# Decoder stack of twelve sections on one core: the attention shift in two bf16 parts instead of three, its selectors in four row tiles, masks behind them, and a new order of turns

## Chip, core and metric

The kernel runs on one NeuronCore of a Trainium2 chip. The metric is the device time of one execution in microseconds; the number given for a kernel is the median of its runs. The kernel before took 4295.11 us (median of 3 runs, 4294.72 to 4298.41).

## What is computed

Input `x` is 32 sequences of 128 tokens of width 128. Four layers follow, each of an attention, a cross attention and a feed-forward part, each behind a layer norm and added to `x`:

```python
x = x + _L0_attn_ref(_layernorm(x, axis=-1), ...)     # delta rule
x = x + _L0_xattn_ref(_layernorm(x, axis=-1), ctx_1024, ctx_1024, ...)   # 16 heads of width 8
x = x + _L0_ffn_ref(...)
x = x + _L1_attn_ref(...)                             # 16 heads, causal
...
x = x + _L2_attn_ref(...)                             # 16 heads, rotary, causal
x = x + _L2_xattn_ref(..., mask_BxSxS2_if1, ...)      # 16 heads, given mask
...
x = x + _L3_xattn_ref(...)                            # 4 heads of width 32
x = x + _L3_ffn_ref(...)
```

The change touches the softmax of five of the twelve sections:

```python
scores = jnp.einsum('bhqd,bhkd->bhqk', q, k) / np.sqrt(HEAD_DIM)
scores = jnp.where(causal[None, None], scores, -jnp.inf)
attn = jax.nn.softmax(scores, axis=-1)
o = jnp.einsum('bhqk,bhkd->bhqd', attn, v)
```

The softmax is made with a shift: the row maximum (over k) is subtracted from the scores before the exponential. Any shift near the maximum gives the same quotient.

## The kernel before

The 32 sequences are worked on in eight groups of four. Two **streams** (0 and 1) take two sequences each (`G = 2`) and run at the same time on the same engines, half a program apart: stream 0 starts a round with section L0_delta, stream 1 with L2_attn. The program has a first stretch (stream 1 alone, sections L0_delta to L1_moe), seven rounds of a hardware loop in which each stream passes all twelve sections, a last stretch (stream 0 with twelve sections, stream 1 with six) and a tail for the experts of the last section.

Each section is written as one generator for each engine. A generator stops at each `yield`. What order the two streams' pieces take on an engine is fixed ahead of time by strings of turns: `TURNS[0]` is PE's string in a round, `LAST_TURNS[0]` that in the last stretch (then ACT's, DVE's, POOL's and SP's). A `0` or `1` runs that stream to its next `yield`; a `w`, on PE only, puts in a **fill**: one bf16 matmul of 256 columns (`warm`, L2432) into a bank that is free anyway, whose result nobody reads. PE has 671 fills in a round and 613 in the last stretch, 7 x 671 + 613 = 5310 in all. The first stretch has none.

`attention16` does the four 16-head attentions. The heads stand as four groups `j` of four heads `i`. For each of the two sequences `s`:

- PE makes the scores `S{s}{j}` (L773: four products, each with 32 rows of the array, so that four stand side by side) and adds the mask as a product with the identity (`masking`, L743 or L746, one of 512 columns for each `j`).
- DVE takes the maxima, negated, into `negm` (L919, four), and splits them into three bf16 parts, each chained to the one before by a semaphore (L923 to L926), into columns 0, 32 and 64 of `mparts`. POOL has cleared `mparts` (L949).
- PE turns `mparts` (L792), ACT copies it to `mT` (L875), PE makes the scores a second time, turned (`T{s}{j}`, L773 again), adds the turned mask, and adds the shift to each head by a **selector** product (L807): the stationary operand is one column of `sel_part`, repeated 128 times, that picks the three rows of head `a` from the 128 rows of `mT`. There are 16 selectors of 128 columns for each `s`.
- ACT takes the exponentials of `T{s}{j}` (L883, four), PE multiplies them with the values and with ones (L823), DVE divides (L931, L932).

I call what is between the maxima of one `s` and its values a **turn of the shift**. A round has 2 streams x 4 sections x 2 sequences = 16 of them in `attention16`, and 4 more in `cross3` (the 4-head attention), which does the same with one group of four heads, one transposition and four selectors: 20 in a round. The first stretch has 4, all in `attention16`; the last has 12 in `attention16` and 4 in `cross3`.

Of the kernel before, what the change touches and what calls it, by code (L numbers as in the profile page):

```python
# [65 lines left out]
    ("w10w1wwwwwwww00www10000w1w0wwwwwwww1wwwwwwwwwwwwwwwwwwwwwwwwwwwwwwwwwww0ww0wwwwwwwwwwwwwwwwwwwwwwwwww10w0ww"  # L66
     "wwwww1wwwwwwwwwwww1www101w0w11www0w1www1w1ww1wwww10w11111w11w0www01www1010w000w0w0w1wwwwwww1ww001wwwww0w01w"
     "w00ww0w00ww1www00ww1111000011110110101011111000100101010111101w010001011w11w1w11w1w1w1111111111110111001011"
     "101110101111111111011011111111100www1w1111110w01011010111ww001ww01000w10www101wwwwww0ww11w01w1www100ww0w0w1"
     "wwww11w11ww01w1ww1wwwww11www10w0111wwww00001www11101w11011011w1w00w1wwww111ww0wwww1wwww1w1w0wwwwww0w11ww101"  # L70
     "0110001101w011011111010011110000101001w0wwwww0ww1w01w0ww1w10w0w00w101w0wwww0ww11w10w00000001001110w00111ww1"
     "0010110w1wwww00ww00010w1000ww01wwwww00w00ww000w0www00www00000www00w000010w0w00wwwwww0w0101111wwww00w0wwwwww"
     "ww100www0wwwwww1ww0100www0w000w1w01011000000w10ww0w0www0wwwwwwwwwwwwwwwwwwwwwwwwwwwwwwwww0wwwww0wwwwwwww100"
     "wwwww1w1ww1w0w0www01110110100000000000001w0011011w11101101101001000100001ww1001100000011011011101000w001111"
     "0011000000000000000000w00w1010100001111000001w01wwww10wwww000001w0www0www1www010w00w0101wwwwwwwwwww11ww011w"
     "www1w10wwwwwwww10w0www1wwwwwwwww1w0w0w1w1w0w1w1ww000w1wwwwww000ww1www1w01wwwwwww0w0w0w0w0ww1001w0w010w00www"
     "wwww11w00ww0ww00ww0w0w01wwwwwwwwww00w0www0w0www1w0w01ww011w0w00ww0w0wwwww000wwww1wwww0w0w00wwwwww0ww0ww0w1w"
     "w0www1www0wwwwww0wwww00w01110111w01w010111010w111w0w1w0011w01w00w1wwwwww1w000w10w00w1w0ww1www0w1w1ww1ww0www"
     "wwww10ww1wwww01wwwwww1w01ww1111101101111101ww1w11111w1w1111111111111111111111111111111"),
    ("01010101000000001101011110111110000100011001010011100101001001010101010000010100011111011111110101111101111"  # L80
     "01001011111100111110111011111100111110111001101111101110011001011100110000011010001011000011001010000100110"
     "00010011101010011000000011111001001101100001010000100000111010101010000000111110111000011010001101100010101"
     "01001100000101111000000001010010000110001001110101100001000000001000110011011001110100010011110100101001100"
     "101101111101101100000110111101110111111111"),
    ("01010101000100111011011101001110111010000000001100000010001110001010100111101010011111001110001010101010110"
     "00001011100100100001111001001110110001010001011101100111111101101101110101111000110011011101101001000101000"
     "01011011111011110111110100101011001101111000011100011110110001010001000000000010010000111000000010010000011"
# [25 lines left out]
     "10010000000010000100000000000101111010010100101110000110000000001110000001011011101111011010101010110011010"  # L113
     "00000000111000111100001110110110000000000001001011100100001100000000011000000001001100000000110100010000000"
     "0001000000000"),
    ("101010000000010100000110000000010100000000111110000100"),
    ("110010"),
]
LENGTHS = 4
# [2498 lines left out]
```

## Time and profile before

| | before |
|---|---|
| median of the runs | 4295.11 us (3 runs, 4294.72 to 4298.41) |
| the profiled execution, its own time | 4291.49 us |
| its span | 4289.5 us |
| PE matmul busy | 3937.5 us, 92% |
| PE weight loads busy | 2841.4 us, 66% |
| DVE busy | 3102.7 us, 72% |
| ACT busy | 1977.8 us, 46% |
| POOL busy | 654.7 us, 15% |
| mean granted clock of TensorE | 0.950 |

PE's ends are modelled, so its busy time is no measure of how full it is; where one instruction begins after another is the better reading. PE's busy time holds the fills. The eight reloads of stream 0's input stand 512.6 us apart (from about 708 to 3783.5 us), which is the length of a round.

### The profile page before, as it was taken

To read this page: it belongs to the slowest core of one execution; us is meant where nothing else is said; L and a number is where in the kernel's file an instruction comes from. 1 tells how busy PE (TensorE), PEld (TensorE's weight loads), DVE (VectorE), ACT (ScalarE), POOL (GpSimd) and SP (SyncE) were. 2 spreads that over 40 slices of the span, in tenths; PEclk is the share of its full clock that TensorE was granted. 3 is DMA by queue.
4 is the path that set the end of the run, shared out by engine and by line. 5 is a ranking of instruction groups with operands and counts; after the bars stand their busy time and mean duration, and the time that the engine had idled before them with its cause. 6 is when DMAs were issued, how large, how long until landed. Compare 5 with 4: busy or idle time off the path is not lost. (4 is left out here: it accounts for less than half of the span.)

```text
span 4289.5 us, 102291 instructions
## 1 busy us (share of the span) xinstructions
PE 3937.5 (92%) x41486; PEld 2841.4 (66%) x41486; DVE 3102.7 (72%) x8220; ACT 1977.8 (46%) x4830; POOL 654.7 (15%) x988
## 2 busy tenths in 40 slices
PE   4799999999999999999999999999999999999998
PEld 3476676766666666666676666776676666666675
DVE  4468777687876868778686886768777687875782
ACT  2254463544535444353534546345453544446551
POOL 2020201102020120211112020120202112120003
PEclk6899999999999999999999999999999999999999
DMA  6000000000000000000000000000000000000003
GB/s 165 1 2 1 9 1 9 2 1 9 1 9 2 9 2 1 10 1 9 2 9 2 1 9 2 9 2 1 9 1 9 2 8 2 2 8 1 1 1 102
DMA packets 52836, 46.15 MB, mean 11 GB/s; under 512 B 8354, under 2 KB 48914, under 8 KB 52126
## 3 DMA queue, kind: packets, MB, share of 16 engines
q1 hardware_dynamic: 48076, 33.04, 2.8%
q8 instruction: 343, 5.62, 0.5%
q0 software_dynamic: 2560, 5.79, 0.4%
q14 instruction: 143, 1.17, 0.1%
q10 hardware_dynamic: 1714, 0.54, 0.1%
HBM read 27.25 MB, written 12.62 MB: 9 GB/s over the span
## 5 line engine op out<-in xcount | busy, mean ns | idle before, releaser
L2432 PE MATMUL banks<-ident_bf 128*128 128x256 bf16 x5310 | 878.8, 278 | 37.1 <-issue 32.7
L2432 PEld LDWEIGHTS banks<-ident_bf 128*128 128x128 bf16 x5310 | 513.6, 101 | 231.9 <-issue 121.0
L883 ACT ACTIVATE scratch<-banks 128x512 f32<-128x512 f32 x512 | 279.5, 598 | 171.5 <-PE banks L807 170.6
L773 PE MATMUL banks<-scratch 32*128 32x512 f32 x2048 | 339.1, 653 | 9.9 <-DVE scratch L932 3.6
L919 DVE TENSOR_REDUCE scratch<-banks 128x4 f32<-128x512 f32 x512 | 323.2, 678 | 14.9 <-PE banks L743 5.4
L341 ACT ACT_TABLE_LOAD x249 | 319.5, 1283 | 27.6 <-PE banks L1100 23.3
L1756 DVE TENSOR_TENSOR_SCAN scratch<-scratch 128x512 f32<-128x512 f32 x256 | 312.7, 1222 | 9.1 <-ACT scratch L1699 3.2
L1699 ACT ACTIVATE scratch<-scratch,ssm_A 128x256 f32<-128x256 f32 x512 | 229.8, 503 | 164.0 <-DVE scratch L1756 162.6
L1611 PE MATMUL banks<-scratch,w_ident 128*128 128x256 f32 x1024 | 271.5, 387 | 19.6 <-DVE scratch L1762 19.6
L598 POOL TENSOR_TENSOR 0_rstd<-0_var,minus_half 128x2 f32<-128x2 f32 x96 | 74.1, 771 | 1303.3 <-DVE 0_var L616 1104.2
L1895 PE MATMUL banks<-scratch 32*32 32x32 f32 x10496 | 234.2, 206 | 33.4 <-issue 26.8
L1895 PEld LDWEIGHTS banks<-scratch 32*32 32x32 f32 x10496 | 201.3, 118 | 85.9 <-issue 62.3
L1237 PE MATMUL banks<-experts,scratch 128*128 128x128 f32 x1792 | 245.9, 283 | 7.9 <-ACT scratch L1273 4.7
L1237 PEld LDWEIGHTS banks<-experts,scratch 128*128 128x128 f32 x1792 | 230.6, 196 | 26.9 <-ACT scratch L1273 10.5
L1273 ACT ACTIVATE scratch<-banks,w_e_b 128x256 f32<-128x256 f32 x448 | 194.2, 474 | 76.4 <-PE banks L1229 70.4
L598 POOL TENSOR_TENSOR 1_rstd<-1_var,minus_half 128x2 f32<-128x2 f32 x96 | 75.1, 782 | 993.7 <-DVE 1_var L616 965.0
L823 PE MATMUL banks<-scratch 128*32 128x128 f32 x4096 | 213.6, 280 | 4.4 <-ACT scratch L883 2.6
L931 DVE RECIPROCAL scratch<-banks 128x128 f32<-128x128 f32 x128 | 122.2, 954 | 130.9 <-PE banks L823 130.0
L1611 PEld LDWEIGHTS banks<-scratch,w_ident 128*128 128x128 f32 x1024 | 177.0, 190 | 54.9 <-DVE scratch L1762 31.9
L807 PEld LDWEIGHTS banks<-scratch,sel_part_bf 128*128 128x128 bf16 x2048 | 152.3, 100 | 87.3 <-issue 21.7
L823 PE MATMUL banks<-scratch,w_slots 128*32 128x128 f32 x4096 | 206.4, 273 | 0.0
L807 PE MATMUL banks<-scratch,sel_part_bf 128*128 128x128 bf16 x2048 | 192.7, 224 | 6.5 <-ACT scratch L875 5.8
(525 smaller groups left out, 8213.9 us busy)
## 6 DMA issues: line engine op xcount, KB each, us to landing
expert_in<-scratch SPq DMA_DIRECT2D x1, 4112.0 KB, 26.6
experts<-in_e_W SPq DMA_DIRECT2D x14, 256.0 KB, 5.6
scratch<-expert_in SPq DMA_DIRECT2D x2, 1542.0 KB, 11.5
w_e_W<-in_e_W SPq DMA_DIRECT2D x3, 704.0 KB
experts<-in_e_w SPq DMA_DIRECT2D x1, 1792.0 KB, 8.7
experts<-in_e_w SPq DMA_DIRECT2D x2, 896.0 KB, 12.9
scratch<-expert_in SPq DMA_DIRECT2D x2, 514.0 KB, 4.4
0_xres<-in_x SPq DMA_DIRECT2D x8, 128.0 KB, 2.1
```

The costliest lines, as they stand in the source:

```text
L341: act.preload_act_table_set(name)
L773: last = pe.matmul(row_tiles(t), lhs[r, col(s)], rhs[r, s], start=True, stop=letter == "S" and mask is None, skip_group_check=True)
L807: last = pe.matmul(t[:, i * L:(i + 1) * L], sel_part[:, a:a + 1].broadcast_to([128, 128]), mT[:, col(s)], start=False, stop=i == NI - 1, s ...
L823: last = pe.matmul(t[32 * i:32 * i + 32, k * L:(k + 1) * L], W["slots"][:, 32 * j:32 * j + 32] if k else vslot[:, s, j, i, :], pT[:, s % 2 ...
L883: P.give(act.activation(pT[:, s % 2, j, :], t, ACT.Exp), f"{nm}.T{s}{j}")
L919: P.give(dve.tensor_reduce(negm[:, s, NI * j:NI * j + NI], row_tiles(t), X, ALU.max, negate=True), f"{nm}.S{s}{j}")
L1237: last = pe.matmul(t[:, col(s)], hid[:, e % RING, c, col(s)], w2[:, 2 * e + c, :], start=c == 0, stop=c == 1, skip_group_check=True)
L1611: last = pe.matmul(total[:, c * N:(c + 1) * N], ident[:], yc[:, k % RING, j, :], start=False, stop=n == DS - 2 and j == 1, skip_group_chec ...
L1699: ins = act.activation(decay[:, k % RING, j, :], dstart[:, c, :], ACT.Exp, scale=ssm_A[:, c, n + j:n + j + 1])
L1756: dve.tensor_tensor_scan(*flat, 0.0, ALU.mult, ALU.add).then_inc(ev(nm + ".state"), 1)
L1895: last = pe.matmul(t[dst, h * width:(h + 1) * width], lhs(h), rhs(h), start=True, stop=True, skip_group_check=True)
L2432: pe.matmul(banks[:, bank, 0:N].rearrange("p (s f) -> p s f", s=G), ident_bf[:], spread(ident_bf[:], G), start=True, stop=True, skip_group ...
```

## The change

- **Two parts, read in place.** `negm` lies in the even places of a float buffer with 16 places of its own for each kind; the upper half of each of its words, read as bf16, is the first part. One DVE operation writes the remainder, rounded to bf16, into the upper half of the word 16 places on. `mparts` is now a view of 32 bf16 columns (stride two). The three other DVE operations, and in `attention16` the clearing on POOL, are gone.
- **Four row groups.** Instead of one transposition of 128 columns, four products with a stationary operand of 32 columns write the same 32 rows into partitions 0 to 31, 32 to 63, 64 to 95 and 96 to 127. ACT's copy to `mT` has the same size.
- **Selectors side by side.** The selectors of group `j` read only rows 32j to 32j+31 (`[32, 128]` stationary); the order is `i` outside, `j` inside, so four neighbours use four different row groups and four different banks. In `cross3` the four selectors use rows 0 to 31 alone.
- **Masks last.** All 16 selectors come ahead of the masks. There is a `yield` between products and selectors, and one ahead of every second mask.
- **Turns placed anew.** All strings of turns are others. PE's has 708 fills in a round (671 before) and 797 in the last stretch (613): 5753 in all, 443 more.

```diff
-    ("w10w1wwwwwwww00www10000w1w0wwwwwwww1wwwwwwwwwwwwwwwwwwwwwwwwwwwwwwwwwww0ww0wwwwwwwwwwwwwwwwwwwwwwwww10w0ww"
...
+    ("11wwwwww0ww0w0w0000w1wwwwwwww0wwwww1wwwwwwww0wwwwww0wwwwwwwwwwwwww1wwwww1w0www00wwwwww1w0wwwwwwwwwww111www"
...
-    c["sel_part"] = ((i[:, :1] % 32 == np.arange(NH)[None, :]) & (i[:, :1] < 96)).astype(np.float32)
+    c["sel_part"] = (i[:, :1] % 16 == np.arange(NH)[None, :]).astype(np.float32)
...
-                    negm, mrest = (S.take(G * NH).rearrange("p (s h) -> p s h", s=G) for _ in range(2))
-                    mparts = S.take(N, BF16).rearrange("p (s f) -> p s f", s=G)
+                    shift_flat = S.take(G * 2 * NH)
+                    negm = shift_flat.rearrange("p (s k h) -> p s k h", s=G, k=2)[:, :, 0, :]
+                    mparts = shift_flat.bitcast(BF16).rearrange("p (s a w) -> p s a w", s=G, w=2)[:, :, :, 1]
...
-                            P.close(pe.transpose(t.bitcast(BF16)[:, 0:L], mparts[:, s, :], ident_bf[:]), f"{nm}.mT{s}")
+                            for j in range(NJ):
+                                last = pe.matmul(t[32 * j:32 * j + 32, 0:L], mparts[:, s, :], ident_bf[:], start=True,
+                                                 stop=True)
+                            P.close(last, f"{nm}.mT{s}")
...
-                            for j in range(NJ):
-                                if j % 2 == 0 and j:
-                                    yield
-                                if mask:
-                                    masking(pe, P.bank(f"{nm}.T{s}{j}"), True, s)
-                                if j == 0:
-                                    P.wait_given(pe, f"{nm}.mT{s}")
-                                t = P.bank(f"{nm}.T{s}{j}")
-                                for i in range(NI):
+                            yield
+                            P.wait_given(pe, f"{nm}.mT{s}")
+                            for i in range(NI):
+                                for j in range(NJ):
                                     a = NI * j + i
-                                    last = pe.matmul(t[:, i * L:(i + 1) * L],
-                                                     sel_part[:, a:a + 1].broadcast_to([128, 128]), mT[:, col(s)],
-                                                     start=False, stop=i == NI - 1, skip_group_check=True)
-                                P.close(last, f"{nm}.T{s}{j}")
+                                    r = slice(32 * j, 32 * j + 32)
+                                    last = pe.matmul(P.bank(f"{nm}.T{s}{j}")[:, i * L:(i + 1) * L],
+                                                     sel_part[r, a:a + 1].broadcast_to([32, 128]), mT[r, col(s)],
+                                                     start=False, stop=mask is None and i == NI - 1, skip_group_check=True)
+                                    if mask is None and i == NI - 1:
+                                        P.close(last, f"{nm}.T{s}{j}")
+                            if mask:
+                                for j in range(NJ):
+                                    if j % 2 == 0:
+                                        yield
+                                    P.close(masking(pe, P.bank(f"{nm}.T{s}{j}"), True, s), f"{nm}.T{s}{j}")
...
-                            q.link(dve.tensor_copy(mparts[:, s, 0:NH], m))
-                            q.link(dve.tensor_tensor(r, m, mparts[:, s, 0:NH], ALU.subtract))
-                            q.link(dve.tensor_copy(mparts[:, s, 32:32 + NH], r))
-                            dve.tensor_tensor(mparts[:, s, 64:64 + NH], r, mparts[:, s, 32:32 + NH],
+                            dve.tensor_tensor(mparts[:, s, NH:2 * NH], negm[:, s], mparts[:, s, 0:NH],
                                               ALU.subtract).then_inc(ev(f"{u}.mparts"), 1)
...
-                        pool.memset(mparts, 0.0).then_inc(ev(f"{u}.ones"), 1)
```

PE's order in the round, at stream 1's first turn of the shift (section L2_attn, causal), before. `scratch1` is stream 1's work space and `scratch0` that of stream 0, which is in L0_delta; `ident_bf 128x256` is the fill.

```order
L792 MATMUL banks<-ident_bf,scratch1 128x128
L2432 MATMUL banks<-ident_bf 128x256 x3
L773 MATMUL banks<-scratch1 128x512 x4
L743 MATMUL banks<-causal_T_bf,ident_bf 128x512
L807 MATMUL banks<-scratch1,sel_part_bf 128x128 x4
L743 MATMUL banks<-causal_T_bf,ident_bf 128x512
L807 MATMUL banks<-scratch1,sel_part_bf 128x128 x4
L1878 MATMUL banks<-scratch0 128x256 x2
L743 MATMUL banks<-causal_T_bf,ident_bf 128x512
L807 MATMUL banks<-scratch1,sel_part_bf 128x128 x4
L743 MATMUL banks<-causal_T_bf,ident_bf 128x512
L807 MATMUL banks<-scratch1,sel_part_bf 128x128 x4
```

The same place of the changed kernel:

```order
L797 MATMUL banks<-ident_bf,scratch1 32x128 x4
L777 MATMUL banks<-scratch1 128x512 x4
L810 MATMUL banks<-scratch1,sel_part_bf 128x128 x16
L2431 MATMUL banks<-ident_bf 128x256 x4
L747 MATMUL banks<-causal_T_bf,ident_bf 128x512 x2
L2431 MATMUL banks<-ident_bf 128x256 x3
L747 MATMUL banks<-causal_T_bf,ident_bf 128x512 x2
```

The transposition has become four products, the 16 selectors stand together right behind the turned products, and the masks, which close the banks for ACT, stand behind four and three fills.

DVE's order at the same place, before (L919 are the maxima; L2104, L2147 and L2158 are stream 0's L0_delta):

```order
L919 TENSOR_REDUCE scratch1<-banks 128x4
L923 CAST scratch1<-scratch1 128x16
L924 TENSOR_TENSOR scratch1<-scratch1 128x16
L925 CAST scratch1<-scratch1 128x16
L926 TENSOR_TENSOR scratch1<-scratch1 128x16
L919 TENSOR_REDUCE scratch1<-banks 128x4
L2104 SCALAR_TENSOR_TENSOR scratch0<-scratch0,w_d_mid_w 128x256 x2
```

and in the changed kernel (L926 are the maxima there, L2103, L2157 stream 0):

```order
L926 TENSOR_REDUCE scratch1<-banks 128x4 x2
L929 TENSOR_TENSOR scratch1<-scratch1 128x16
L2103 SCALAR_TENSOR_TENSOR scratch0<-scratch0,w_d_mid_w 128x256 x2
L2157 TENSOR_TENSOR scratch0<-banks,w_delta_masks 128x256
```

Four small operations have become one, and what follows them is another piece of the other stream.

## Rows read from the trace of the kernel before

**Rows 1.** The page's first part: busy time, share of the span, instructions

```profile
span 4289.5 us, 102291 instructions
PE 3937.5 (92%) x41486; PEld 2841.4 (66%) x41486; DVE 3102.7 (72%) x8220; ACT 1977.8 (46%) x4830; POOL 654.7 (15%) x988
```

**Rows 2.** Busy time of each engine in stretches: first, a round, last, tail

```profile
core 0: us, PE busy (x) PEld busy (x) DVE busy (x) ACT busy (x) POOL busy (x), PEclk, DMA share, GB/s
10.00:195.00 185.00, 104.92 (x1262) 74.79 (x1263) 86.76 (x264) 49.94 (x137) 29.64 (x43) 0.67 0.35 90
...
708.00:1221.00 513.00, 483.11 (x5156) 348.35 (x5155) 384.80 (x1023) 243.28 (x600) 78.48 (x118) 0.96 0.02 5
...
3784.00:4205.00 421.00, 389.33 (x3766) 282.38 (x3764) 301.41 (x767) 210.60 (x472) 47.93 (x74) 0.96 0.04 12
```

**Rows 3.** The same stretches, the fills (L2432) alone

```profile
708.00:1221.00 513.00, 112.14 (x671) 64.77 (x671) 0.96 0.02 5
3784.00:4205.00 421.00, 93.61 (x592) 58.77 (x593) 0.96 0.04 12
```

**Rows 4.** Two of twenty equal pieces of a round, all engines

```profile
733.60:759.20 25.60, 25.05 (x263) 15.03 (x264) 24.07 (x61) 10.16 (x29) 7.92 (x9) 1.00 0.01 2
...
784.80:810.40 25.60, 24.27 (x303) 18.94 (x291) 10.15 (x34) 11.60 (x33) 0.69 (x1) 0.80 0.01 1
```

**Rows 5.** Timeline, first stretch: start us, us, engine, line

```profile
123.63 0.17 DVE L923 CAST scratch<-scratch 128x16 bf16<-128x16 f32 x1
...
124.25 0.17 DVE L926 TENSOR_TENSOR scratch<-scratch 128x16 bf16<-128x16 f32 x1
...
130.50 1.07 PE L807 MATMUL banks<-scratch,sel_part_bf 128*128 128x128 bf16 x16
130.94 2.07 ACT L883 ACTIVATE scratch<-banks 128x512 f32<-128x512 f32 x4 [1.13 <-PE banks L807]
131.59 0.16 PEld L823 LDWEIGHTS banks<-scratch 128*32 128x32 f32 x8 [0.20 <-ACT scratch L883]
```

**Rows 6.** Groups by line and shape, whole span: busy us, mean ns

```profile
L875 ACT COPY scratch<-banks 128x128 bf16<-128x128 bf16 x128 | 33.6, 262 | 289.0 <-PE banks L792 287.9
...
L923 DVE CAST scratch<-scratch 128x16 bf16<-128x16 f32 x128 | 26.5, 207 | 4.4
L924 DVE TENSOR_TENSOR scratch<-scratch 128x16 f32<-128x16 f32 x128 | 25.1, 196 | 4.4
...
L949 POOL MEMSET scratch<- 128x256 bf16 x64 | 20.2, 315 | 0.0
```

**Rows 7.** Timeline of a masked turn in a round

```profile
1171.03 1.14 PE L773 MATMUL banks<-scratch 32*128 32x512 f32 x8
...
1172.11 0.39 PE L743 MATMUL banks<-causal_T_bf,ident_bf 128*128 128x512 bf16 x1
...
1172.33 0.39 PE L807 MATMUL banks<-scratch,sel_part_bf 128*128 128x128 bf16 x4
...
1172.56 0.38 PE L743 MATMUL banks<-causal_T_bf,ident_bf 128*128 128x512 bf16 x1
...
1172.76 2.06 ACT L883 ACTIVATE scratch<-banks 128x512 f32<-128x512 f32 x4 [3.61 <-PE banks L807]
```

**Rows 8.** Timeline: starts in column tiles, fills, 32 by 32 tiles

```profile
1175.78 0.40 PE L823 MATMUL banks<-scratch 128*32 128x128 f32 x8
...
1176.00 0.40 PE L823 MATMUL banks<-scratch,w_slots 128*32 128x128 f32 x8
...
1176.34 0.28 PE L2432 MATMUL banks<-ident_bf 128*128 128x256 bf16 x1
...
1006.50 3.92 PEld L2432 LDWEIGHTS banks<-ident_bf 128*128 128x128 bf16 x36
...
782.54 1.61 PE L1895 MATMUL banks<-scratch 32*32 32x32 f32 x112
784.08 0.43 PE L823 MATMUL banks<-scratch 128*32 128x128 f32 x8
```

More of the change, by code:

```diff
@@ L743, in masking @@
                             last = pe.matmul(v, ident_bf[:], spread((causal_T_bf if turned else causal_bf)[:], NI),
-                                             start=False, stop=not turned, skip_group_check=True)
+                                             start=False, stop=True, skip_group_check=True)
                         if mask == "given":
                             last = pe.matmul(v, ident_root[:], spread((maskT_bf if turned else mask_bf)[:, s, :], NI),
-                                             start=False, stop=not turned, skip_group_check=True)
+                                             start=False, stop=True, skip_group_check=True)
                         return last
@@ L874, in act_f @@
                             t = P.take(act, f"{nm}.mT{s}")
-                            P.give(act.copy(mT[:, col(s)], t.bitcast(BF16)[:, 0:L]), f"{nm}.mT{s}")
+                            P.give(act.copy(mT[:, col(s)], t[:, 0:L]), f"{nm}.mT{s}")
                             if s >= 2:
@@ L1402, in cross3 @@
                     qz, kz = (S.take(G * H3 * L).rearrange("p (s h t) -> p s h t", s=G, h=H3) for _ in range(2))
-                    negm, mrest = (S.take(G * H3).rearrange("p (s h) -> p s h", s=G) for _ in range(2))
-                    mparts_flat = S.take(N, BF16)
-                    mparts = mparts_flat.rearrange("p (s f) -> p s f", s=G)
+                    shift_flat = S.take(G * 2 * NH)
+                    negm = shift_flat.rearrange("p (s k h) -> p s k h", s=G, k=2)[:, :, 0, 0:H3]
+                    mparts = shift_flat.bitcast(BF16).rearrange("p (s a w) -> p s a w", s=G, w=2)[:, :, :, 1]
                     mT = S.take(N, BF16)
@@ L1446, in turned @@
                             for h in range(H3):
-                                last = pe.matmul(t[:, h * L:(h + 1) * L], sel_part[:, h:h + 1].broadcast_to([128, 128]),
-                                                 mT[:, col(s)], start=False, stop=h == H3 - 1, skip_group_check=True)
+                                last = pe.matmul(t[:, h * L:(h + 1) * L], sel_part[0:32, h:h + 1].broadcast_to([32, 128]),
+                                                 mT[0:32, col(s)], start=False, stop=h == H3 - 1, skip_group_check=True)
                             P.close(last, f"{nm}.T{s}")
```

116 lines of the change are left out of this document (57 added, 59 removed).

## Prediction

> **What bounds the kernel now.** I read the page's totals first. PE is busy 92% of the span, DVE 72%, ACT 46% [rows 1]. That makes PE the first suspect, but its 92% holds the fills, so the next view is the stretches. A round takes 513 us, with PE busy 483.1 and DVE 384.8 [rows 2]; seven of them are 3588 us of the span. Then the fills by themselves: 671 in a round [rows 3]. A run of 36 of them begins its loads within 3.92 us, so one costs PE 0.109 us [rows 8], and 671 are 73 us. So a round is, in PE's order, about 410 us of work, 73 us of fills and 30 us in which nothing runs (513 - 483). The fills stand where a wait was expected. They are slack turned into instructions: PE has some 20% of room on average, and the two streams' chains set the end as much as PE does.
>
> Two of twenty equal pieces of a round show both kinds [rows 4]. In the first, DVE is busy 24.1 of 25.6 us: DVE sets the pace, and PE is padded. In the second DVE is busy 10.2 us and PE 24.3, at a granted clock of 0.80, which means that a part of it ran at 1.2 instead of 2.4 GHz: there PE binds. In the whole view of twenty pieces, of which two stand there, DVE is over 23.4 of 25.6 us in five, and 92 of the round's 256 selectors (36%) fall in these. So a turn of the shift is in the DVE-bound part in about one case of three.
>
> **The change part by part.**
>
> *DVE.* Alone on the engine, the first and the fourth of the four operations begin 0.62 us apart [rows 5]: 0.207 us from one to the next, of which the operation is 0.17 and the rest the chain of semaphores. In the mean over the program they are 0.19 to 0.21 us each [rows 6]. Three of four go: 0.62 us for each turn. With 20 turns a round that is 12.4 us of DVE's 385, and 0.62 us of each stream's own chain ten times a round. The one operation left reads with a stride; bounds for it are 0.17 us (the row) and twice that, and I take 0.17.
>
> *PE, selectors.* Sixteen in a row begin at 130.50 and the next product begins at 131.59, of which ACT's wait is 0.20 [rows 5]: 0.89 us, 0.055 each. Between two masks four selectors take 0.23 us [rows 7], the same. In four tiles side by side, eight instructions of 128 columns begin every 0.22 us, 0.027 each [rows 8], at 1175.78 and 1176.00; with tiles of 32 by 32, 112 of 32 columns take from 782.54 to 784.08, 0.014 each [rows 8]. So 16 selectors in four row tiles take between 0.23 us (0.014 each) and 0.44 us (0.027 each), if they run side by side at all, and 0.89 if not. The turned products of the same shape, 32 rows by 128, do run side by side: four of 512 columns in float32 take from 1171.03 to 1172.11, 1.08 us [rows 7], while one mask of 512 columns in bf16 takes 0.22. I take 0.33, the middle: 0.56 us less for each of the 16 turns, 9.0 us a round. The four turns in `cross3` use one row tile for all four selectors and save nothing on PE.
>
> *PE, the turned parts.* One transposition becomes four products in column tiles. Four side by side cost no more than one (0.027 against 0.055 each), but the array changes its tiling once more. From the last group in column tiles at 1176.00, plus its 0.22, to the fill at 1176.34 are 0.12 us in which nothing begins [rows 8]. With one or two more such changes for each turn I take 0.18 us, 3.6 us a round for 20 turns. Bounds: nothing (where values stand right ahead, in column tiles too) and 0.24.
>
> The Trainium skill, page "TensorEngine Tiling (Array Packing)", section Key Properties, says that a change of the tiling mode drains the array, not only a change of tile. By that rule, the trace agrees: the 0.12 us is what it costs here, and it speaks against this edit. The Trainium skill, page "TensorE: Matmul & The Clock Gate", section Part 1, puts a floor of about 25 ns from one start to the next. The trace differs, with 0.014 us in 32 by 32 tiles. By the page's floor, 16 selectors would be 0.40 us, and the saving 7.8 instead of 9.0 us a round.
>
> *PE, masks last.* The same masks, four of 0.22 us; only their place moves. The saving of 0.2 us that a mask gave as cover while ACT copies `mT` (0.262 us, [rows 6]) is gone, but the products, 1.08 us, cover the copy alone. What this does to ACT's first exponential is the rival below.
>
> *POOL.* 64 clearings of 0.315 us go [rows 6]. POOL is busy 15% of the span [rows 1]; worth nothing. Cover gone, it would be 0.3 us for each section, 8 a round.
>
> *Fills.* 37 more in a round: 37 x 0.109 = 4.0 us of PE. In the last stretch 184 more, 20 us, if they fell on work and not on waits.
>
> **The sum.** PE's account of a round: -9.0 + 3.6 + 4.0 = -1.4 us, if the 30 us of unfilled waits stay. DVE's account: -12.4 us. The truth lies between, by who binds where. A third (36%) of the turns lies where DVE binds, 4.5 us, and I count half of that as gained, since PE's fills already stand in the new order for the rest: -2.2. A round then changes by -3.6 us, seven by -25. In the first stretch stream 1 is alone and has four turns, each with one of the two savings (0.62 or 0.56) on its chain: -2. In the last stretch PE's account is 12 x -0.56 + 16 x 0.18 + 20 = +16 us; were all 184 fills free, it would be -4. The stretch had 421 - 389 = 32 us of unfilled waits [rows 2] which more fills can take up, so I set +4. The tail has none of this. Together -25 - 2 + 4 = -23 us. The profiled execution took 4291.5 us (span 4289.5), the median of the runs is 4295.1, 3.6 more; a difference is carried over to the median as it is. **4295.1 - 23 = 4272 us**, 0.5% faster. About 0.2% (8.6 us) is what a measurement of this kernel tells from no change, so 4286 and 4304 are the borders.
>
> **Rivals.**
>
> *B, DVE's whole saving comes through.* If a round is set by the streams' chains over DVE, the fills are free and 12.4 us a round come off: 7 x 12.4 = 87, 2 in the first stretch, 16 x 0.62 = 10 in the last: 99 us, 4196 us. For it: DVE at 24.1 of 25.6 us in such pieces [rows 4], and fills of 73 us a round that only mark waits [rows 3]. Against it: the piece at 0.80, where DVE is busy 40% only, and that PE's order is fixed, so that a wait saved on DVE is gained only if PE's next item is ready. Its own range is 4170 to 4240.
>
> *C, nothing comes of it.* PE's account with the selectors at their bound of 0.44 us and two tile changes (0.24) is -7.2 + 4.8 + 4.0 = +1.6 us a round, 11 in seven rounds; the gain on DVE of 2.2 a round takes 15 off: -4 us, 4291, inside the border. For it: the number of fills rose, so the plan found more waiting, not less.
>
> *D, slower: ACT's exponentials begin later.* Before, the first bank is closed by one mask and four selectors, 0.45 us behind the products, and ACT begins at 1172.76 [rows 7]. After, it waits for all 16 selectors (0.33), a tile change (0.12) and a mask (0.22): 0.67 us, and where the order puts four fills between (as at the first turn of the round), 0.44 more. ACT's four exponentials (2.07 us in a row, [rows 5]) and then the values come behind. The delay is 0.22 to 0.66 us on the chain that DVE's 0.62 shortens. It decides from 0.62 us on. If an item of the other stream the size of four products (1.08) comes between, a turn loses 0.22 + 1.08 - 0.62 = 0.7 us; with a stream's eight turns a round 5.4 us, 38 in seven rounds: 4333 us. For it: the two new stops between selectors and masks. Against: in unmasked sections (4 of 16 turns) there is no mask to wait for, and the last of the four banks is ready earlier than before (1.33 us behind the products instead of 1.8), which ACT's pace of 0.5 us for each bank hardly uses.
>
> Single pieces could go so too: the clock falls to 1.2 GHz in parts of a round (0.96 in the mean, [rows 2]); fewer selectors or more fills shift where, worth a few us a round to either side. That is in the ranges.
>
> **Chances.** The forecast (about 4250 to 4286) 0.42; B 0.20; C 0.17; D 0.21. Faster by over 0.2%: 0.62, the forecast and B. Within: 0.17. Slower: 0.21. For the range I leave out half of B below (under 4200) and half of D above (over 4325): 4200 to 4325. The likeliest case's own range is 4250 to 4286.
>
> **What the profile after would show.** Selectors: 16 begin within 0.23 to 0.44 us; at 0.89 the side-by-side step is wrong. DVE: one operation of 0.17 us a turn, DVE's busy time down by 160 x 3 x 0.19, some 90 us, to about 3010. Tile changes: a gap of about 0.12 us ahead of and behind the four turned products. Fills: 708 a round, and the unfilled waits of a round near 30 us; if they fall to 25 or below, the gain is B's, if they rise to 35 or more, D's. ACT: its idle time ahead of the exponentials (L883; 1.13 us ahead of the four of [rows 5], 3.61 ahead of those of [rows 7]) up by 16 x 8 x 0.2 or more speaks for D. The stretches: a round near 509 us, the last stretch 415 to 430. The prediction fails if the new order, not the edit, decides: a round that changes by more than 10 us with the single durations as given here.

## The result: 0.4% slower

The changed kernel takes 4310.6 us (median of 20 runs, 4302.0 to 4327.9); the kernel before, on the same chip, 4295.0 (20 runs, 4289.0 to 4304.4). The ratio is 1.004, with a 95% interval of 1.003 to 1.0049: slower by some 16 us where 23 us less were forecast. The profiled execution took 4322.7 us, the second longest of the 20 and 12 us above their median; that of the kernel before, 4291.5, was 3.6 below its own.

The page of the changed kernel, first the totals that answer to [rows 1], then groups with the line, busy time, mean ns of one, and idle time ahead of them:

```profile
span 4320.6 us, 103424 instructions
...
PE 3940.2 (91%) x42313; PEld 2812.0 (65%) x42313; DVE 3005.1 (70%) x7740; ACT 2049.9 (47%) x4890; POOL 670.5 (16%) x924
...
L2431 PE MATMUL banks<-ident_bf 128*128 128x256 bf16 x5753 | 958.1, 279 | 51.0 <-issue 33.0
...
L344 ACT ACT_TABLE_LOAD x279 | 358.0, 1283 | 24.9 <-PE banks L1102 20.7
L892 ACT ACTIVATE scratch<-banks 128x512 f32<-128x512 f32 x512 | 277.4, 601 | 146.2 <-PE banks L747 106.4
```

DVE's busy time went down by 98 us as forecast, to 3005. PE's stayed (3937.5 before), with 443 more fills in it. So PE's idle time, span less busy, rose from 352 to 380 us. ACT has 30 more loads of its function tables in this group (249 before), and 60 more in all groups together (337, 277 before). The stretches that answer to [rows 2] (first, a round, last), all engines:

```profile
10.00:200.00 190.00, 110.03 (x1292) 79.38 (x1293) 86.38 (x256) 50.72 (x139) 28.51 (x41) 0.64 0.35 88
714.00:1228.00 514.00, 480.68 (x5231) 341.99 (x5230) 372.60 (x962) 252.43 (x607) 77.91 (x110) 0.96 0.02 5
3796.00:4232.00 436.00, 402.81 (x3975) 290.56 (x3973) 289.12 (x712) 214.85 (x472) 47.73 (x69) 0.96 0.03 9
```

From one load of `0_xres` to the next the round takes 513.6 us (512.6 before; seven loads, not eight, stand that far apart), and the last stretch, from the last load to the last store of the output, 436.4 (419.7 before). Of the 31 us between the two profiled spans, 4.6 are in the first stretch, 7.5 in seven rounds, 16.7 in the last stretch and 2.3 behind it. The medians are only 16 us apart: this pair of executions shows where time went, but overstates how much. In a round PE waits 33.3 us unfilled (514.00 - 480.68), 30 before.

The timeline of the changed kernel in the first stretch (start, us, engine, line), then in a round:

```profile
123.43 0.18 DVE L929 TENSOR_TENSOR scratch<-scratch 128x16 bf16<-128x16 f32 x1
...
130.78 0.26 PE L797 MATMUL banks<-ident_bf,scratch 128*32 128x128 bf16 x4
...
130.96 1.14 PE L777 MATMUL banks<-scratch 32*128 32x512 f32 x8
...
131.93 0.40 PE L810 MATMUL banks<-scratch,sel_part_bf 32*128 32x128 bf16 x16
```

```profile
1172.76 1.14 PE L777 MATMUL banks<-scratch 32*128 32x512 f32 x8
...
1173.83 0.28 PE L2431 MATMUL banks<-ident_bf 128*128 128x256 bf16 x1
...
1174.05 0.23 PEld L810 LDWEIGHTS banks<-scratch,sel_part_bf 32*128 32x128 bf16 x16
1174.05 0.40 PE L810 MATMUL banks<-scratch,sel_part_bf 32*128 32x128 bf16 x16
...
1174.38 0.39 PE L1625 MATMUL banks<-scratch,sel_state_bf 96*128 96x256 bf16 x2
...
1174.72 0.59 PE L747 MATMUL banks<-causal_T_bf,ident_bf 128*128 128x512 bf16 x2
...
1175.14 0.60 ACT L892 ACTIVATE scratch<-banks 128x512 f32<-128x512 f32 x1 [4.53 <-PE banks L747]
1175.15 0.38 PE L1625 MATMUL banks<-scratch,sel_state_bf 96*128 96x256 bf16 x2
...
1175.38 0.59 PE L747 MATMUL banks<-causal_T_bf,ident_bf 128*128 128x512 bf16 x2
```

One DVE operation is left, of 0.18 us. The weight loads of all 16 selectors fit in 0.23 us, 0.014 each: they lie side by side, at the lower bound that was given. The next product begins 0.33 us behind the first selector (1174.05 to 1174.38), just the price that was taken; in the other 15 turns of that round it is 0.33 to 0.40. The single pieces cost what was predicted. But the two places at which PE now hands over are used: pieces of the other stream (L1625) stand between selectors and masks and between the masks.

### The profile page after: what moved, and what is told of

It is laid out like the page before. It is cut to its first block and busy times, and to the rows that moved or that the text cites. A ratio compares the mean times of both kernels' runs of the same rounds, so it can differ in the third digit from the quotient of the medians.

```text
span 4320.6 us, 103424 instructions
## 1 busy us (share of the span) xinstructions
PE 3940.2 (91%) x42313; PEld 2812.0 (65%) x42313; DVE 3005.1 (70%) x7740; ACT 2049.9 (47%) x4890; POOL 670.5 (16%) x924
## 5 line engine op out<-in xcount | busy, mean ns | idle before, releaser
L2431 PE MATMUL banks<-ident_bf 128*128 128x256 bf16 x5753 | 958.1, 279 | 51.0 <-issue 33.0
L2431 PEld LDWEIGHTS banks<-ident_bf 128*128 128x128 bf16 x5753 | 555.0, 101 | 304.7 <-issue 136.4
L344 ACT ACT_TABLE_LOAD x279 | 358.0, 1283 | 24.9 <-PE banks L1102 20.7
L892 ACT ACTIVATE scratch<-banks 128x512 f32<-128x512 f32 x512 | 277.4, 601 | 146.2 <-PE banks L747 106.4
L926 DVE TENSOR_REDUCE scratch<-banks 128x4 f32<-128x512 f32 x512 | 322.7, 679 | 31.8 <-PE banks L750 11.9
L777 PE MATMUL banks<-scratch 32*128 32x512 f32 x2048 | 315.0, 653 | 9.7 <-DVE scratch L919 9.2
L1239 PE MATMUL banks<-experts,scratch 128*128 128x128 f32 x1792 | 246.6, 283 | 18.4 <-ACT scratch L1275 15.5
L1239 PEld LDWEIGHTS banks<-experts,scratch 128*128 128x128 f32 x1792 | 234.5, 197 | 40.1 <-ACT scratch L1275 25.1
L1275 ACT ACTIVATE scratch<-banks,w_e_b 128x256 f32<-128x256 f32 x448 | 196.7, 475 | 56.3 <-PE banks L1231 52.6
L606 ACT COPY 0_hT<-banks 128x256 f32<-128x256 f32 x96 | 35.8, 373 | 335.8 <-PE banks L596 334.7
L1625 PE MATMUL banks<-scratch,sel_state_bf 96*128 96x256 bf16 x1024 | 189.7, 273 | 0.1
```

Of the source, the lines that this page charges most:

```text
L344: act.preload_act_table_set(name)
L777: last = pe.matmul(row_tiles(t), lhs[r, col(s)], rhs[r, s], start=True, stop=letter == "S" and mask is None, skip_group_check=True)
L892: P.give(act.activation(pT[:, s % 2, j, :], t, ACT.Exp), f"{nm}.T{s}{j}")
L926: P.give(dve.tensor_reduce(negm[:, s, NI * j:NI * j + NI], row_tiles(t), X, ALU.max, negate=True), f"{nm}.S{s}{j}")
L1239: last = pe.matmul(t[:, col(s)], hid[:, e % RING, c, col(s)], w2[:, 2 * e + c, :], start=c == 0, stop=c == 1, skip_group_check=True)
L1275: P.give(act.activation(hid[:, e % RING, c, :], t, ACT.Gelu, bias=W["e2_b1"][:, 2 * e + c:2 * e + c + 1]), f"{nm}.u{e}.{c}")
```

## Experiments

Twelve kernels ran, with 4 to 12 timed runs each. They ran in four sets on different chips, in which the kernel before took 4296.7 to 4304.1 us, so sets are compared by ratios to it; the interval behind each ratio is one of 95%. "Old order" means the strings of turns of before, and PE's pieces cut as these strings need them; "new order" means the strings of the change with its two new stops of PE, the one behind the turned products and the one behind the selectors. Strings and stops were not tried apart.

**1. The whole edit in the old order.** The code of the change with the strings of before (one line of each stands in the diff); products, selectors and the first two masks stand in one piece of a turn, the other two masks in the next.

```diff
-    ("11wwwwww0ww0w0w0000w1wwwwwwww0wwwwww1wwwwwwww0wwwwww0wwwwwwwwwwwwww1wwwww1w0www00wwwwww1w0wwwwwwwwwww111www"
+    ("w10w1wwwwwwww00www10000w1w0wwwwwwww1wwwwwwwwwwwwwwwwwwwwwwwwwwwwwwwwwww0ww0wwwwwwwwwwwwwwwwwwwwwwwwww10w0ww"
...
-                            yield
                             P.wait_given(pe, f"{nm}.mT{s}")
```

> The whole edit (two parts, four row groups, selectors side by side, masks behind the selectors) in the turns of the kernel before: all five strings are before's, the two new stops of PE are left out so that the pieces fit (selectors stand in one piece with the products, masks 0 and 1 behind them, masks 2 and 3 in the next piece). Theory O (the new order of turns and its fills cost the time, the edit itself gains): my own sum without the fills, -5.4 us a round on PE and up to -12.4 on DVE, gives 4235 to 4275 us, likeliest 4255, and the last stretch stays at 415 to 420 us. Theory E (the edit itself costs, because ACT's first exponential starts later or TensorE's clock falls more often): 4300 us or more in the old turns too, and the round is over 513 us.

4241.3 us (4235.9 to 4248.7), ratio 0.9869 (0.9852 to 0.9886). It is faster than both kernels. The edit is worth 56 us, 8.6 in each round (503.9 us); the sign of the result comes from the new order.

**2. The other way round: the parts of before in the new order.**

```diff
-                            for j in range(NJ):
-                                last = pe.matmul(t[32 * j:32 * j + 32, 0:L], mparts[:, s, :], ident_bf[:], start=True,
-                                                 stop=True)
-                            P.close(last, f"{nm}.mT{s}")
+                            P.close(pe.transpose(t.bitcast(BF16)[:, 0:L], mparts[:, s, :], ident_bf[:]), f"{nm}.mT{s}")
```

> The reverse: the new kernel's five strings of turns and its pieces on PE (stops between products, selectors and masks), with three parts, four chained DVE operations, one transposition and full-array selectors as in the kernel before. Theory O: this is the dearest of the four, 4295 + 7 x (4.0 fills + 1 to 2 of drift) + 20 in the last stretch or more, 4335 to 4370 us, last stretch 440 us or more. Theory E: near the kernel before, 4290 to 4305 us.

4424.7 us, ratio 1.0299 (1.0281 to 1.0318), dearer than either theory said. With the edit's parts the new order costs 73 us (1.004 - 0.9869). With the old parts it is 128, but this kernel keeps the masks behind its 16 full-array selectors too, so the 128 are not the order alone. The edit's parts help in both orders: 56 us in the old one, 111 in the new one (1.0299 - 1.004).

**3. Fewer fills in the last stretch.** The changed kernel, 184 fills taken from the longest runs of the last strings; the diff has the beginning of PE's string (w is a fill).

```diff
-wwww1ww00wwwwww0w0000ww110ww1wwwwww1wwwwww0
+wwww1ww00wwww0w0000ww110ww1wwww1wwww0
```

> The new kernel, in the last stretch 184 of its 797 fills left out (the longest runs shortened to at most five), so that it has the 613 of the kernel before; all other turns stay. Theory F (fills of the last stretch lie on PE's path; PE's account of +16 us is right): 15 to 20 us come off, 4290 to 4296 us, and the last stretch falls from 436 to 416 to 421. Theory W (they stand in waits, the order of the work sets the stretch): within 3 us of the new kernel, 4308 to 4314. Theory C (they hold TensorE at 2.4 GHz): slower than the new kernel, 4315 or more, with more time at 1.2 GHz in the last stretch.

4322.0 us, ratio 1.0055 (1.0034 to 1.0076), no less than the changed kernel's 1.004; the last stretch takes 436.3 us without them and 436.4 with them. In this order the fills of the last stretch cost nothing.

**4. DVE's part alone, old order.** One operation instead of four and four column products, but 16 selectors over the full array, and the masks where they were.

```diff
-                                                     sel_part[r, a:a + 1].broadcast_to([32, 128]), mT[r, col(s)],
+                                                     sel_part[:, a:a + 1].broadcast_to([128, 128]), mT[:, col(s)],
```

> DVE's part of the edit alone in the turns of the kernel before: two parts read in place, one DVE operation; PE makes four small column products instead of the transposition and then the 16 full-array selectors one after another, each behind its mask as before (selector rows beyond 32 are zero). Theory D (the chain over DVE counts, as half of my gain assumed, 2.2 us a round or more): 4295 - 16 to 60, 4235 to 4280 us. Theory P (only PE's account counts): the column products and tile changes cost up to 3.6 us a round, 4295 to 4320 us.

4301.2 us, ratio 1.0005 (0.9992 to 1.0017). Its page has PE busy 3958.5 us, 21 more than before (0.13 us for each of 160 turns, where I had set 0.18). The time is that of the kernel before: what the shorter chain gives is no more than what the column products take.

**5. The selectors' part alone.** Experiment 1 with DVE's chain as long as before: three idle operations ahead of the one.

```diff
+                            q.link(dve.tensor_copy(idle[:, s, :], negm[:, s]))
+                            q.link(dve.tensor_tensor(idle[:, s, :], negm[:, s], idle[:, s, :], ALU.subtract))
+                            q.link(dve.tensor_copy(idle[:, s, :], idle[:, s, :]))
```

> The whole edit in the order of before, but VectorE's chain between the column products and ScalarE's copy is kept as long as it was: three idle 16-wide operations, each reading what the one ahead wrote, stand ahead of the one addition in each turn (they move no number of the result). Theory P (the gain of 58 us comes from TensorE's selectors lying side by side, since VectorE's part alone was worth nothing): 4238 to 4256 us. Theory N (both parts are needed: with the selectors short, VectorE's chain is what a turn waits for, so that its three operations cost what they take): up to 140 turns times 0.45 us = 63 us more, 4270 to 4305 us, nothing left of the gain.

4260.0 us, ratio 0.9894 (0.9879 to 0.9908), between the two theories. 46 of the 56 us stay; DVE's three operations in 160 turns (busy 3095.7 us against 3010.7, 85 more) are worth some 11. The two ratios' intervals overlap a little (that of experiment 1 ends at 0.9886), so the 11 is rough. The 46 are what the selectors and the masks' new place bring together.

**6. Masks ahead of the selectors.** Experiment 1 with the four masks ahead.

```diff
+                            if mask:
+                                for j in range(NJ):
+                                    masking(pe, P.bank(f"{nm}.T{s}{j}"), True, s)
                             P.wait_given(pe, f"{nm}.mT{s}")
```

> The whole edit in the order of before, but the four masks are put ahead of the 16 selectors, where they were before the change, not behind them. Theory M (masks last matters: exponentials of a bank begin only when its selector group is done, and masks last let the short group end each bank): 4250 to 4275 us, as a turn's first bank closes earlier or later by some 0.2 us in 140 turns. Theory S (only the sum of TensorE's work counts): 4236 to 4247 us, as e1's 4241. Faster than 4236 us would say that the masks close banks later in e1 than the selectors do here.

4274.1 us, ratio 0.9929 (0.9913 to 0.9945), 26 us more. The exponentials in experiment 1, then the same group here (last numbers: ACT's idle time ahead of them, and what ended it):

```profile
L888 ACT ACTIVATE scratch<-banks 128x512 f32<-128x512 f32 x512 | 278.2, 599 | 157.7 <-PE banks L744 112.0 <-PE banks L747 39.4 <-PE banks L806 3.5
```

```profile
L887 ACT ACTIVATE scratch<-banks 128x512 f32<-128x512 f32 x512 | 276.3, 602 | 227.7 <-PE banks L809 226.1
```

And the same turn in both timelines, experiment 1 first:

```profile
1164.12 1.14 PE L774 MATMUL banks<-scratch 32*128 32x512 f32 x8
...
1165.08 0.40 PE L806 MATMUL banks<-scratch,sel_part_bf 32*128 32x128 bf16 x16
...
1165.41 1.04 PE L744 MATMUL banks<-causal_T_bf,ident_bf 128*128 128x512 bf16 x4
...
1165.84 2.07 ACT L888 ACTIVATE scratch<-banks 128x512 f32<-128x512 f32 x4 [3.70 <-PE banks L744]
```

```profile
1167.41 1.14 PE L774 MATMUL banks<-scratch 32*128 32x512 f32 x8
...
1168.48 1.04 PE L744 MATMUL banks<-causal_T_bf,ident_bf 128*128 128x512 bf16 x4
...
1169.45 0.40 PE L809 MATMUL banks<-scratch,sel_part_bf 32*128 32x128 bf16 x16
...
1169.88 2.07 ACT L887 ACTIVATE scratch<-banks 128x512 f32<-128x512 f32 x4 [4.45 <-PE banks L809]
```

ACT begins 1.72 us behind the first product with the masks last, 2.47 with them ahead. In the kernel before, where masks and selectors alternate bank by bank, it was 1.73 [rows 7]. When the selectors are short and go over all banks at once, masks last closes the first bank three of its four masks earlier, and so keeps ACT's start where it was. Without that, the edit in the old order is worth 31 us (1 - 0.9929) and not 56, though PE's busy time is nearly the same (3893.3 us, 3886.0 in experiment 1).

**7. More fills in the old order.** Experiment 1 with one fill more in each of the 37 longest runs of a round, and 184 more in the last stretch: as many fills as the changed kernel has (beginning of PE's string).

```diff
-w10w1wwwwwwww00www10000w1w0wwwwwwww1
+w10w1wwwwwwwww00www10000w1w0wwwwwwwww1
```

> The whole edit in the order of before, with 37 fills more in each of the seven rounds and 184 more in the last stretch, one each added to the longest runs of fills. Prices what the fills of the new order cost where the order is the old one. Theory F (a fill costs its 0.109 us wherever it stands): seven times 4.0 and 20, 4289 us. Theory W (fills go into waits that are there anyway, or pay for themselves in clock): 4225 to 4255 us. In between: the share of them on the path, by (time - 4241) / 48.

4270.5 us, ratio 0.9924 (0.9911 to 0.9938): 24 us for 443 fills, half of what they take at 0.109 us each (48 us). The profiled last stretch grows by 12 us, from 421.7 to 433.7.

**8. Fewer fills in the new order.** The changed kernel with 671 fills a round and 613 in the last stretch, the numbers of before (beginning of PE's string).

```diff
-11wwwwww0ww0w0w0000w1wwwwwwww0wwwwww1wwwwwwww0ww
+11wwwwww0ww0w0w0000w1wwwwwww0wwwwww1wwwwwww0www
```

> The changed kernel with 37 fills fewer in each of the seven rounds (671, as many as before the change) and 184 fewer in the last stretch (613), taken one by one from the longest runs of fills. With the edit in the order of before (old order, few fills: ratio 0.9869), the same with more fills (old order, many: 0.9924) and the changed kernel (new order, many: 1.004) it fills the fourth cell. Theory H (fills cost the same in either order, 0.0055 of the time, and the order the rest): ratio 0.9985, some 4288 us. Theory O (the new order needs its fills, for the clock and since its waits are longer): 1.002 to 1.008, 4304 to 4330 us. Theory X (the new order is as good as the old one once it has as few fills): 0.987 to 0.991, 4240 to 4257 us.

4316.4 us (4299.6 to 4341.8), ratio 1.0036 (1.002 to 1.0052), the same as the changed kernel's 1.004. Taking the fills back brings nothing back; had they cost what they cost in the old order, the ratio would be 0.9985, outside the interval. The profiled execution, 4299.6 us, was the shortest of the 12. The totals of experiment 7 (old order, many fills), then of this one (new order, few):

```profile
span 4262.9 us, 103365 instructions
...
PE 3923.4 (92%) x42313; PEld 2812.5 (66%) x42313; DVE 3013.1 (71%) x7740; ACT 1972.2 (46%) x4830; POOL 645.9 (15%) x924
```

```profile
span 4297.7 us, 102538 instructions
...
PE 3876.8 (90%) x41870; PEld 2751.6 (64%) x41870; DVE 3004.2 (70%) x7740; ACT 2046.4 (48%) x4890; POOL 671.0 (16%) x924
```

**9 and 10. No fills at all**, in the old order and in the new one.

```diff
-                    warm(args[0], P)
+                    pass
```

> The whole edit in the old turns with no fill at all (5310 of 256 columns less, 579 us of PE at 0.109 each). Theory P (fills are work on PE's path, at least in part): faster than 4241. Theory W (they only pad waits, and keep TensorE at 2.4 GHz): slower, by up to half of the time that then passes at 1.2 GHz; with 1500 us at that clock instead of 399 some 100 to 400 us more, 4340 to 4640.

> The new kernel with no fill at all. Against the run before it, which has the old turns and no fills either: theory F (the 443 more fills are the cost of the new turns): the distance of 69 us falls to 20 or less. Theory O (the order of the other work is): it stays at 50 us or more.

Old order 4291.7 us, ratio 0.9994 (0.9976 to 1.0011); new order 4393.2 us, ratio 1.022 (1.02 to 1.0241). Between them lie 97 us with not one fill in either: the order costs by itself. The fills earn their place: without them the mean granted clock of the profiled executions falls from 0.952 to 0.877 and from 0.945 to 0.855, and the time grows by 54 and 77 us by the ratios. The 4291.7 us lie between the two theories.

**11 and 12. No changes of ACT's table**, in the new order and in the old one. The new order has 60 more loads of ACT's function tables, so I thought that these were its price. The expectations count 323 and 271 loads; these are the two largest groups, and all groups together have 337 and 277. Both kernels leave out SiLU, GELU and the logarithm, and 10 loads remain in each.

```diff
-EXP, SILU, GELU, LN = "exp_and_others", "silu_and_others", "gelu_and_others", "natural_log"
+EXP = SILU = GELU = LN = "exp_and_others"
...
-                            P.give(act.activation(z[:, c, :], t, ACT.Silu), f"{nm}.in{2 + c}")
+                            P.give(act.activation(z[:, c, :], t, ACT.Identity), f"{nm}.in{2 + c}")
```

> The new kernel with no change of ACT's table: Silu, Gelu and Ln are replaced by Identity, which changes what is computed, and only the Exp table is ever loaded. Order, fills and all operands stay. The new turns make ACT load a table 323 times in the profiled run, the old ones 271 times, 1.283 us each: 52 more, 66.7 us of ACT, and the new turns cost 69 us (4310.6 against 4241.3). Theory T (the additional table loads stand on the chain and are the cost of the new turns): the new kernel falls further than its counterpart with the old turns, and the distance of the two falls from 69 us to 20 or less. Theory R (the order of the work itself, on PE and DVE, is the cost): the distance stays at 50 to 70 us. Absolute: 4150 to 4270 us.

> The counterpart: the whole edit in the old turns, Silu, Gelu and Ln replaced by Identity, only the Exp table loaded. Theory T: 20 us or less below the run before it. Theory R: 50 to 70 us below it. Absolute: 4100 to 4220 us.

New order 4253.5 us, ratio 0.9906 (0.9886 to 0.9927); old order 4190.7 us, ratio 0.9747 (0.9727 to 0.9767). The distance stays: 68 us without the loads, 73 with them. That theory fell. The 60 loads more, 77 us of ACT's time, are worth some 5 us, too few to tell from nothing with intervals of 9 us to either side.

## Why the prediction was wrong

The ratios side by side, all with the edit's parts (in the last row each order has its own number of fills, 5310 and 5753):

| | old order | new order | new less old |
|---|---|---|---|
| no fills | 0.9994 | 1.022 | 0.023, 97 us |
| fills as before | 0.9869 | 1.0036 | 0.017, 72 us |
| fills as changed | 0.9924 | 1.004 | 0.012, 50 us |
| no table changes | 0.9747 | 0.9906 | 0.016, 68 us |

**The step that failed** is the one on the turns: the new strings were priced by their fills alone, "37 x 0.109 = 4.0 us of PE", and the order itself at nothing ("if the 30 us of unfilled waits stay"). Measured, the order costs 50 to 97 us, whatever the fills, where the sum had nothing. In the totals of the pages PE's time divides so (idle is span less busy; the clock is the mean granted one of the same execution):

| | busy | idle | clock |
|---|---|---|---|
| before | 3937.5 | 352.0 | 0.950 |
| edit, old order | 3886.0 | 350.5 | 0.952 |
| changed kernel, fewer fills | 3876.8 | 420.9 | 0.951 |
| edit, old order, more fills | 3923.4 | 339.5 | 0.950 |
| changed kernel | 3940.2 | 380.4 | 0.945 |
| no fills, old order | 3575.6 | 710.7 | 0.877 |
| no fills, new order | 3669.9 | 740.2 | 0.855 |
| no table changes, old order | 3869.8 | 321.7 | 0.955 |
| no table changes, new order | 3906.1 | 340.9 | 0.956 |

Each new order has more idle time of PE than its old one, but idle time is not the whole price. With as many fills as in the change, the profiled executions are 58 us apart: 41 more idle and 17 more busy. With few fills idle time grows by 70, more than the 61 us by which the executions differ, and without table changes by 19 of 56. With no fills it is 30 of 124 us; the other 94 are busy time for the same work, at a lower clock. By the clock, 0.855 and 0.877 mean 1279 and 1054 us at 1.2 GHz (twice the missing share, times the span). For the pair with as many fills this is no steady reason: the changed kernel's 0.945 belongs to that one execution, the median over its 20 runs is 0.950, as in experiment 7, and by the ratios the two are 50 us apart, not 58.

Where PE waits, the view of PE's waits says (line that waits, what it waited for: us, times, longest). Changed kernel:

```profile
PE banks L596 <- DVE 1_hn L624: 52.0, 43, 16.7
...
PE banks L596 <- DVE 0_hn L624: 24.1, 31, 2.0
PE banks L637 <- ACT scratch L2078: 21.5, 8, 3.1
...
PE banks L1239 <- ACT scratch L1275: 15.5, 10, 1.8
...
PE banks L1610 <- DVE scratch L1761: 1.2, 3, 0.5
```

Edit in the old order, the same places, and two more that wait for the same SiLU (L2074):

```profile
PE banks L593 <- DVE 1_hn L621: 45.5, 29, 16.9
...
PE banks L1606 <- DVE scratch L1757: 19.6, 30, 1.0
PE banks L593 <- DVE 0_hn L621: 14.5, 30, 0.8
...
PE banks L1227 <- ACT scratch L2074: 6.1, 7, 1.1
...
PE banks L1235 <- ACT scratch L1271: 4.7, 7, 1.5
...
PE banks L1235 <- ACT scratch L2074: 2.2, 7, 0.3
...
PE banks L634 <- ACT scratch L2074: 1.6, 2, 0.8
```

The reader is to see many small waits that move, in places that the edit doesn't touch. The norms' results (L624) come later for 6.5 and 9.6 us more. The wait for the router's SiLU is now one of 21.5 us, 2.7 in each of eight places; in the old order it is 9.9 us in three places. The expert layer waits 15.5 instead of 4.7 us for ACT's GELU (L1275). Another wait is nearly gone: the one for DVE's product behind the scan (L1757, L1761 in the changed kernel), 19.6 us in the old order and 1.2 in the new.

How an order makes such a wait is seen in a round of the changed kernel. ACT makes one SiLU of stream 0's router (L2078), then a GELU of stream 1's experts (L1275), then the two other SiLUs, and loads a table at each turn from one to the other. PE has eight products of stream 1 to do in between (L1239) and then stands idle for 2.94 us:

```profile
813.81 0.47 ACT L2078 ACTIVATE scratch<-banks,w_d_r_b 128x256 f32<-128x256 f32 x1
...
814.30 1.28 ACT L1275 ACT_TABLE_LOAD   x1
...
814.38 1.16 PE L1239 MATMUL banks<-experts,scratch 128*128 128x128 f32 x8
815.59 0.47 ACT L1275 ACTIVATE scratch<-banks,w_e_b 128x256 f32<-128x256 f32 x1
...
816.09 1.28 ACT L2078 ACT_TABLE_LOAD   x1
817.38 0.84 ACT L2078 ACTIVATE scratch<-banks,w_d_r_b 128x256 f32<-128x256 f32 x2
...
818.48 0.60 PE L637 MATMUL banks<-w_d_r_b,ones_row 1*128 1x32 f32 x2 [2.94 <-ACT scratch L2078]
```

These two waits are not the price of the order, though. Without the table changes (experiment 11) they fall from 21.5 and 15.5 us to 0.8 and 3.0, and the distance of the two orders is still 68 us. So the list of waits says what the order moves and not what it costs. That the new order is the cause is shown; which engine's string holds it, or whether PE's two new stops do, is not. Strings of one engine from the old order beside others from the new one weren't tried. What put the strings in this order is also open.

**PE's account of the edit** was right in PE's busy time. From experiment 4 to 1 it falls by 72.5 us, 0.57 for each of the 128 turns with four groups (0.56 said); the column products cost 0.13 a turn (0.18 said). The measured -51.5 us in eight rounds is -6.4 a round, where -9.0 + 3.6 = -5.4 was said. In time, experiment 4 to 1 is 58 us (1.0005 - 0.9869), where the selectors' term, 0.56 in 128 turns, was 72. Of the 58, 33 come with the masks ahead (experiment 6) and 26 by the masks' place, which was priced at nothing. Since masks ahead of short selectors let ACT begin 0.74 us later than in the kernel before, the 33 are no price of the selectors alone.

**DVE's credit** of 2.2 us a round was near: some 11 us in all (experiment 5), 1.4 a round, far from the 12.4 of DVE's own account. Rival B, all of DVE's saving on the path, is out. So without its strings the edit was forecast at -7.6 us a round, and it measures -8.6. That the two are so close is in part luck: the selectors with the masks' place brought less than the sum had, and DVE's part with the column products, 1.4 us a round dearer by the sum, cost nothing that could be measured (experiment 4).

**The first and the last stretch.** The first took 4.6 us more, within what it moves from one profile to another (195.6 before, 200.2 after, 191.2 to 208.0 in the others), though it has neither strings of turns nor fills. The last was set at +4, with 32 us of waits to take up the fills. It took +17. Experiment 3 shows that in the new order its 184 fills cost nothing, less than was set. The edit in the old order has 421.7 us in it with few fills and 433.7 with many (experiment 7); the new order has 432.3 (experiment 8) or 436.3 (experiment 3) with few and 436.4 with many. So by these profiles, one execution each, the order costs some 11 to 15 us there with few fills and 3 with many: the prices of fills and order do not add.

**Rival D** (ACT's exponentials begin later) ends on the right side, at 4333 us, by the wrong mechanism. ACT's idle time ahead of them fell from 171.5 us to 146.2, and experiment 6 shows that masks last is worth 26 us beside masks ahead. The delay of 0.22 us that it reckoned for the first bank does not show in the old order: ACT begins 1.72 us behind the first product, 1.73 before. What it said of foreign pieces is seen in the timeline: in the masked turn shown, ACT begins 2.38 us behind the first product, against 1.72 in the old order. That one turn is no count of them, and that ACT's idle time ahead of the exponentials is shorter in all speaks against them as the cause.

**Rival C** (nothing comes of it) was near in time, 4291, since the gain of the edit (56 us) and the loss by the order (73) nearly cancel; its reason, selectors at their dear bound, was not.

**The condition of failure** was named, "the new order, not the edit, decides", but the sign to look for was not right: a round that changes by more than 10 us. It changed by 1, as two changes of -8.6 and +9.7 lie in it. The other sign, unfilled waits of a round at 35 us or more, was not reached either (33.3).

## What to carry to other kernels

When a change replaces both the work and a written-out order, the order is a second change of its own size: give it a term with both signs, and run the edit in the old order, which here was 1.7% faster than the changed kernel and 1.3% faster than the one before. Removed busy time is no price by itself. On DVE, 85 us of it were worth some 11; on PE, 72 us (experiment 4 to 1) were worth 58, of which 26 came by moving the masks, with PE's busy time changed by 7 us. Do not take the longest waits of one trace for the cost: two waits of 37 us together all but went away with the table changes, and the orders stayed as far apart.

## What the runs showed of the hardware

- Sixteen bf16 selectors of 128 columns in four row tiles begin within 0.23 us, 0.014 each, half of the 0.027 of the column tiles in float32 [rows 8]. The Trainium skill, page "TensorE: Matmul & The Clock Gate", section Part 1, has a floor of about 25 ns from start to start, however few the columns; for these row tiles the trace differs, and the measurement decides.
- Fills that compute nothing are worth 54 and 77 us here, and the granted clock is higher with them (0.952 against 0.877, 0.945 against 0.855); 443 more of them cost 24 us in one order and nothing that could be measured in the other.
- A table load of ACT takes 1.283 us. The Trainium skill, page "ScalarE: Activation LUTs", section What ACT_TABLE_LOAD costs, gives 1283 ns, and the trace agrees. The section adds a drain of about 1.38 us for every change of table; the trace above differs, with the activation ahead ending at 816.06 (815.59 + 0.47), the load at 816.09 and the next activation at 817.38. Taking out 267 loads in the old order or 327 in the new one (343 or 420 us of ACT) gains 52 or 57 us.
